# Recurrent part of a decoder: full three-pass output product, second norm and shifted term on ScalarE, channel mix added by an accumulating DMA

## The reference

```python
x = layernorm(x, ln0_w, ln0_b)
for l in range(4):
    h = layernorm(x, ln1_w[l], ln1_b[l]); hh = time_shift(h)
    xk, xv, xr = (h * t + hh * (1 - t) for t in (tmk[l], tmv[l], tmr[l]))
    k, v, sr = xk @ Wk[l].T, xv @ Wv[l].T, sigmoid(xr @ Wr[l].T)
    x = x + (sr * wkv(time_decay[l], time_first[l], k, v)) @ Wo[l].T
    h = layernorm(x, ln2_w[l], ln2_b[l]); hh = time_shift(h)
    xk, xr = (h * t + hh * (1 - t) for t in (cmk[l], cmr[l]))
    kf = square(relu(xk @ Wck[l].T))                  # 256 -> 1024
    x = x + sigmoid(xr @ Wcr[l].T) * (kf @ Wcv[l].T)  # 1024 -> 256
```

## Time and profile before

| | |
|---|---|
| runs | median 1903.39 us of 3 (1900.92 to 1904.49) |
| profiled execution | 1903.27 us, its span 1901.6 us |
| mean granted clock of PE | 0.97 of 2.4 GHz |
| busy in the span | PE 93%, PEld (weight loads) 80%, DVE 65%, ACT 44%, POOL 0% |

### The profile page before, as it was taken

How to read it: one execution, slowest core, us unless ns; L and a number is a source line. 1 busy time by engine, 2 the same in 40 slices (tenths; PEclk the granted TensorE clock), 3 DMA queues, 4 the chain that set the end, 5 groups by cost and what they waited for, 6 DMA issues and landing times.

```text
span 1901.6 us, 26356 instructions
## 1 busy us (share of the span) xinstructions
PE 1777.8 (93%) x10124; PEld 1527.4 (80%) x10124; DVE 1233.4 (65%) x1953; ACT 841.2 (44%) x1304; POOL 3.6 (0%) x26
## 2 busy tenths in 40 slices
PE   2399999999999988889799999999999999999997
PEld 1277787877787767788789899889998898998896
DVE  6889999989999943788644445445445444454445
ACT  3465676665667634344332333333333323333333
POOL 0000000000000000000000000000000000000000
PEclk9699999999999998899899999999999999999999
DMA  3000001001001002111021111011100001011001
GB/s 111 5 23 17 10 25 40 6 8 43 17 12 50 1 0 88 52 43 37 10 77 34 34 34 34 0 33 33 33 33 0 33 33 33 33 34 38 1 1 39
DMA packets 35274, 56.54 MB, mean 30 GB/s; under 512 B 3094, under 2 KB 20476, under 8 KB 34684
## 3 DMA queue, kind: packets, MB, share of 16 engines
q1 hardware_dynamic: 35196, 55.47, 9.0%
HBM read 51.79 MB, written 3.67 MB: 29 GB/s over the span
## 4 chain that ended last, share of the span: by engine, by line
PE 49%; DVE 1%; ACT 0%; issue 0%; ACTq 0%; DVEq 0%
PE fbanks L1662 16%; PE fbank L1662 16%; PE fbank L1678 16%; DVE acc L1517 0%; DVE fst L1543 0%; PE fbank L52 0%; DVE xk L1541 0%; ACT acc L1633 0%; PE fbanks L1695 0%; ACT acc L1610 0%; DVE fmv L1546 0%; DVE fyy L1557 0%; DVE frstd L1558 0%; DVE fyy L1556 0%; ACTq L1340 0%
## 5 line engine op out<-in xcount | busy, mean ns | idle before, releaser
L1493 DVE TENSOR_TENSOR hf<-sil,fbanks 128x512 f32<-128x512 f32 (+1 forms) x128 | 79.4, 620 | 332.1 <-PE fbanks L1662 273.4
L1601 ACT ACTIVATE sil<-fbanks 128x512 f32<-128x512 f32 (+1 forms) x128 | 69.6, 544 | 442.2 <-PE fbanks L1662 442.2
L1678 PE MATMUL fbank<-wl,hh 128*128 128x256 f32 x896 | 250.3, 279 | 0.0
L1678 PE MATMUL fbank<-wh,hl 128*128 128x256 f32 x896 | 250.1, 279 | 0.0
L1678 PE MATMUL fbank<-wh,hh 128*128 128x256 f32 x896 | 250.1, 279 | 0.0
L1493 DVE TENSOR_TENSOR hf<-sil,fbank 128x512 f32<-128x512 f32 (+1 forms) x128 | 79.5, 621 | 149.8 <-PE fbank L1662 142.8
L715 PE MATMUL pair<-wcv,kf 128*112 128x256 f32 x768 | 176.1, 379 | 0.0
L1678 PEld LDWEIGHTS fbank<-wl,hh 128*128 128x128 f32 x896 | 168.3, 188 | 2.2
L1678 PEld LDWEIGHTS fbank<-wh,hh 128*128 128x128 f32 x896 | 168.4, 188 | 1.8
L1678 PEld LDWEIGHTS fbank<-wh,hl 128*128 128x128 f32 x896 | 168.4, 188 | 0.0
L1500 DVE TENSOR_TENSOR hl<-hf,hh 128x512 fp32r<-128x512 f32 (+1 forms) x256 | 158.3, 618 | 0.0
(11 more groups left out here) (237 smaller groups left out, 3478.3 us busy)
## 6 DMA issues: line engine op xcount, KB each, us to landing
raw<-in_w_gate SPq DMA_DIRECT2D x16, 512.0 KB, 3.8
raw<-in_w_up SPq DMA_DIRECT2D x16, 512.0 KB, 4.7
raw<-in_w_down SPq DMA_DIRECT2D x16, 512.0 KB, 5.6
raw<-in_w_ck SPq DMA_DIRECT2D x4, 1024.0 KB, 4.8
wcv<-in_w_cv SPq DMA_DIRECT2D x4, 768.0 KB, 4.4
raw<-in_ctx_t SPq DMA_DIRECT2D x4, 750.0 KB, 6.4
ct<-in_ctx_t SPq DMA_DIRECT2D x4, 750.0 KB, 5.0
x<-in_x SPq DMA_DIRECT2D x4, 448.0 KB, 6.2
```

Source lines behind the costliest of these rows:

```text
L1493: dve.tensor_tensor(hf[i][:, 0:w], sil[i][:, 0:w], bank[2 * i + 1][:, 0:w], ALU.mult).then_inc(hf_ready, 1)
L1601: act.activation(sil[f % 2][:, 0:w], bank[2 * (f % 2)][:, 0:w], ACT.Silu).then_inc(sil_ready, 1)
L1678: ins = pe.matmul(bank[4 + 2 * (t % 2) + i // 2][:, (i % 2) * C:(i % 2 + 1) * C], a[t % 2][:, f, i * P:(i + 1) * P], m[h][:, DOWN + f * C: ...
```

## The change

- The output product takes three passes over all eight blocks, and its loop goes by pairs of blocks instead of by sequences: two of the four pairs, the first turn, two pairs. All four `hidden` groups get a high part on ACT and a low part on DVE; `w_cv` goes through the stage buffer as a whole, and half its value is what is split.
- The second norm's four scalings move from DVE to ACT (`normalise(2, ...)`, with a shift computed by DVE).
- The difference of the second mix is gone: ACT writes the previous token's term (`past`, scaled by `1 - mu`), and DVE adds the present token's in one op each (`mix2`).
- `add_channel` is gone: GpSimd issues an accumulating DMA of `cth` onto the tokens, and the semaphore `x_done` counts by 16. ACT's `gate` of the next step and DVE's statistics of the first norm wait for it.
- On ACT, DVE and PE the order changes: `wkv_numerator` moves ahead of the first mix, and the splits of the weights move to other places of a layer's first step.

Its core, in the order GpSimd, SP, DVE, ACT, PE:

```diff
+            for m in range(STEPS):
+                c = m % GROUPS
+                pool.wait_ge(cq_done, 2 * (m + 1))
+                pool.dma_start(x[:, c * G:(c + 1) * G, :], cth[:], accum_op=ALU.add).then_inc(x_done, 16)
...
                 w = io["w_" + name][l].rearrange("p b c -> p (b c)")
-                if name == "cv":
-                    w = w[:, 0:SPLIT * C]
                 sp.dma_start(stage[:, 0:w.shape[1]], w).then_inc(stage_in, 16)
...
             for s in range(-3, STEPS + 1):
                 if valid(s):
                     after(add_wkv(s))
                     stats(2, chunk(s))
-                    if s % GROUPS == 0:
-                        l = s // GROUPS
-                        low_weights(2 * l, wckl, wckh, ck_done, 4 * GROUPS * l)
+                if valid(s - 1):
+                    low_kf(s - 1, 3)
                 if valid(s + 1):
                     wkv_denominator(s + 1)
                 if valid(s):
                     rsqrt(2, s)
-                    normalise(2, xn[2], chunk(s), xn_ready[2])
+                    set_shift(2)
+                if valid(s + 1):
+                    wkv_numerator(s + 1)
                 if valid(s + 2):
-                    n = difference(1, s + 2)
-                    mix(1, s + 2, ("k", "v", "r"), ("tmk", "tmv", "tmr"), mix1_ready, n)
+                    mix1(s + 2)
                 if valid(s):
-                    n = difference(2, s)
-                    mix(2, s, ("cr",), ("cmr",), mix2_ready, n)
+                    mix2(s, 0, "cr", "cmr")
                 if valid(s - 1):
                     gate_channel(s - 1)
                 if valid(s):
-                    mix(2, s, ("ck",), ("cmk",), mix2_ready, n)
-                if valid(s + 1):
-                    wkv_numerator(s + 1)
-                if valid(s - 1):
-                    add_channel(s - 1)
+                    mix2(s, 1, "ck", "cmk")
                 if valid(s):
                     low_ck(s)
+                    if s % GROUPS == 0:
+                        l = s // GROUPS
+                        low_weights(2 * l, wckl, wckh, ck_done, 4 * GROUPS * l)
...
-                if valid(s) and s % GROUPS == 0:
-                    l = s // GROUPS
-                    low_weights(2 * l + 1, wcvl, wcvh, cv_done, 2 * GROUPS * l)
...
                 if valid(s):
                     low_kf(s, 0)
+                if valid(s):
+                    low_kf(s, 1)
+                if valid(s + 2):
+                    wkv_sums(s + 2)
+                if valid(s):
+                    if s % GROUPS == 0:
+                        l = s // GROUPS
+                        low_weights(2 * l + 1, wcvl, wcvh, cv_done, 2 * GROUPS * l)
+                    low_kf(s, 2)
...
+            def past(m, i, name, mu):
+                act.wait_ge(h_ready[2], CB * (m + 1))
+                if m:
+                    act.wait_ge(*((cr_done, m) if name == "cr" else (ck_done, 4 * m)))
+                for b in range(CB):
+                    act.activation(mixed[name][:, b], h[2][:, b, :, 0:T], ACT.Copy, scale=param(m, b, mu))\
+                        .then_inc(past_ready, 1)
...
                 act.wait_ge(square_done, 4 * m + j + 1)
-                if m and j == 0:
-
-                    act.wait_ge(cv_done, 2 * m)
-                act.activation(kfh[:, 2 * j:2 * j + 2], t[:], ACT.Copy).then_inc(kfh_ready, 1)
+                act.activation(kfh[:, 2 * j:2 * j + 2], t, ACT.Copy).then_inc(kfh_ready, 1)
...
                 if valid(s):
                     gate(s)
+                    if s % GROUPS == 0:
+                        l = s // GROUPS
+                        high_weights(2 * l + 1, wcvh, cv_done, 2 * GROUPS * l)
...
-            def channel_out(m, sequences):
...
+            def channel_out(m, pairs):
+                for p in pairs:
+                    pe.wait_ge(kfl_ready, FT // 2 * m + p + 1)
+                    for i in range(G):
+                        for f in range(2):
+                            j = 2 * p + f
+                            for n, (a, w) in enumerate(((kfh[:, j], wcvh), (kfh[:, j], wcvl), (kfl[p][:, f], wcvh))):
+                                ins = pe.matmul(pair[3][0:T, i // 2, (i % 2) * C:(i % 2 + 1) * C],
+                                                a[:, i * T:(i + 1) * T], w[:, j * C:(j + 1) * C],
+                                                start=j == n == i % 2 == 0,
+                                                stop=j == FT - 1 and n == 2 and i % 2 == 1)
...
                     pe.wait_ge(wlo_ready, 2 * (m // GROUPS) + 2)
-                    pe.wait_ge(w_in["cv"], 16 * (m // GROUPS + 1))
                     pe.wait_ge(cth_ready, m + 1)
-                    channel_out(m, (0, 1, 2))
+                    channel_out(m, (0, 1))
...
-                    channel_out(m, (3,))
+                    channel_out(m, (2, 3))
```

More of the change, by code:

```diff
@@ L103, in rwkv_phase @@
         wckh, wckl = sb("wckh", [P, CB * F], F32R), sb("wckl", [P, CB * F], F32R)
-        wcvh, wcvl = sb("wcvh", [P, SPLIT * C], F32R), sb("wcvl", [P, SPLIT * C], F32R)
-        wcv = sb("wcv", [P, (F // P - SPLIT) * C])
+        wcvh, wcvl = sb("wcvh", [P, FT * C], F32R), sb("wcvl", [P, FT * C], F32R)
         prm = sb("prm", [P, L, CB, NPRM])
@@ L137, in rwkv_phase @@
         bb = sb("bb", [P, CB, G, T1])
[L138 to L140 removed]
+        ckh = sb("ckh", [P, CB, G * T], F32R)
+        with nc.sbuf_tensor("mix_ck", [P, CB, G, T], FP32) as t:
+            mixed["ck"] = t
+        ckl = sb("ckl", [P, CB, G * T], F32R)
+        with nc.sbuf_tensor("kf", [P, FT, G * T], FP32) as t:
+            kf = [t[:, 2 * j:2 * j + 2] for j in range(FT // 2)]
+        t = sb("kfl", [P, FT, G * T], F32R)
+        kfl = [t[:, 2 * j:2 * j + 2] for j in range(FT // 2)]
+        kfh = sb("kfh", [P, FT, G * T], F32R)
         cth = sb("cth", [T, G, C])
@@ L407, in low_weights @@
                     dve.wait_ge(used, count)
-                dve.tensor_tensor(tile[:], stage[:, 0:tile.shape[1]], high[:], ALU.subtract).then_inc(wlo_ready, 1)
+                dve.scalar_tensor_tensor(tile[:], stage[:, 0:tile.shape[1]], 0.5 if n % 2 else 1.0, high[:], ALU.mult,
+                                         ALU.subtract).then_inc(wlo_ready, 1)
             def gate_channel(m):
@@ L621, in _ @@
                 if valid(s):
+                    past(s, 1, "ck", "pmk")
+                    if s % GROUPS == 0:
+                        l = s // GROUPS
+                        high_weights(2 * l, wckh, ck_done, 4 * GROUPS * l)
                     high_ck(s)
@@ L699, in hidden @@
                 ins.then_inc(ck_done, 1)
-            def channel_out(m, sequences):
-                for i in sequences:
-                    n = 0
-                    for j in range(F // P):
-                        if i == 0 and j % 2 == 0 and j < SPLIT:
-                            pe.wait_ge(kfl_ready, SPLIT // 2 * m + j // 2 + 1)
-                        elif i == 0 and j % 2 == 0:
-                            pe.wait_ge(square_done, 4 * m + j // 2 + 1)
-                        if j < SPLIT:
-                            parts = [(a[:, j], w[:, j * C:(j + 1) * C]) for a, w in ((kfh, wcvh), (kfh, wcvl), (kfl, wcvh))]
-                        else:
-                            parts = [(kf[j // 2][:, j % 2], wcv[:, (j - SPLIT) * C:(j - SPLIT + 1) * C])]
-                        for a, w in parts:
-                            ins = pe.matmul(pair[3][0:T, i // 2, (i % 2) * C:(i % 2 + 1) * C], a[:, i * T:(i + 1) * T],
-                                            w, start=n == 0, stop=j == F // P - 1)
-                            n += 1
-                    if i % 2:
-                        ins.then_inc(cv_done, 1)
+            def channel_out(m, pairs):
[9 more added lines that the diff above has]
+                                                stop=j == FT - 1 and n == 2 and i % 2 == 1)
+                        if i % 2 and p == FT // 2 - 1:
+                            ins.then_inc(cv_done, 1)
             for s in range(-3, STEPS + 1):
```

154 lines of the change are left out of this document (69 added, 85 removed).

## The result

The changed kernel takes 1936.05 us (median of 4 runs, 1933.73 to 1936.81), the kernel before 1903.94 in the same comparison; the ratio is 1.0169, 95% interval 1.0151 to 1.0186. The profiled execution took 1933.73 us with a span of 1931.6, 30.0 more than the span before.

The account below looks back on a forecast made before the run. PE (TensorE) alone was taken to set the 40.52 us recurrent step. From 1903.27 us, nine ordinary steps -4.2, four layer starts +36 and ends -0.7 gave 1934 us, own range 1918 to 1948 (1911 to 1968 with part of the rivals).

Parts of the forecast that it names:

- The turn comes late: First turn, ordinary step: PE waits 1.4 us for ScalarE's `xn`, so the step takes 40.05 instead of 40.52 us.
- the product's saving: Output product on PE: 1.85 us less work per step, of which an ordinary step keeps only 0.47.
- The second turn holds by 0.2: Second turn: second norm's `xn` ready at H + 26.8, PE there at H + 27.0, so moving that norm costs nothing.
- The DMA is hidden: Accumulating DMA of `cth`: taken as 6.2 us, hidden up to 7.7 us in ordinary steps.
- The layer starts: Weight splits at a layer's first step, four times: the main cost, +9.0 us per layer, +36 in four.
- H': H is the first matmul of a step's hidden product; H' is the next step's, put at H + 40.05.
- the load: The 1 MB `wcv` load at a layer start: 4.8 us, landing at H' + 3.9, ScalarE waiting for it at `wcvh`.
- the half product: Half of the output product, 5.7 us; after PE's wait at a layer start its slower records add 2.4.
- PE's wait for `wcvl`: Output product at a layer start: PE wants `wcvl` at H' + 13.3, ready at H' + 21.9, a stall of 8.6 us.
- Ordinary steps: Nine recurrent steps without a layer start: 0.47 us less each, -4.2 in all.
- the fill: First steps of the recurrent part: PE waits for VectorE anyway, so the change there is 0.
- the ends: Fill 0, last three steps -1.9 us each, +5 at the very end waiting for the DMA: together -0.7.

Follow-up runs that it names:

- experiment 7: Changed kernel with only the order within a step altered on ScalarE and VectorE, shortening the chains to both turns; weight splits stay: 1914.73 us.
- experiment 5: Changed kernel with each accumulating DMA followed by a plain one of the same size into unused memory: 1970.58 us.
- experiment 6: Changed kernel with `xn` of the first norm made ahead of the two `eu` operations on ScalarE, nothing else moved: 1943.03 us.
- experiment 4: Changed kernel without the accumulating DMA; VectorE adds the channel mix's result to the tokens again: 1928.32 us.
- experiment 1: Changed kernel with the low split of the `wcv` weights (`wcvl`) on VectorE moved ahead of the first hidden group's low part: 1923.05 us.
- experiment 2: Changed kernel with an own stage buffer for the `wcv` weights, loaded early; order on every engine stays: 1924.36 us.
- experiment 3: Changed kernel with the own `wcv` stage buffer and `wcvl` ahead of the first hidden group's low part: 1909.58 us.
- experiment 10: Changed kernel with experiments 1, 2, 7 and 8 together, and the last of sixteen accumulating DMAs replaced by two VectorE adds: 1872.45 us, ratio 0.9832.
- experiment 11: On top of experiment 10, the `wcv` low split made by GpSimd in two operations instead of by VectorE: 1894.15 us.
- experiment 8: On top of experiment 3, ScalarE makes the `wcv` high split (`wcvh`) right behind `ckh` instead of behind the gate: 1907.97 us.

## Why the prediction was right, and where it was not

The mechanism was right in its parts, and the time, 1934 against 1936.05, closer than its terms were.

*The turn comes late.* Forecast: a wait of 1.4, a step of 40.05. Measured 1.3 and 40.05. That the product's saving is real is shown by experiment 7, that ScalarE's chain eats it by 5 and 6.

*The second turn holds by 0.2.* `xn` of the second norm ends at 397.93 in the ordinary step that begins at 380.96, PE takes it at 397.98: 0.05 is left over, and in experiment 6 PE waits there.

*The DMA is hidden.* Taken as 6.2 us, it lands after 5.2; in ordinary steps no one waits for it, and experiment 4 changes no step. The fit in the Trainium skill (DMA: Bandwidth & Descriptors, Anatomy of one DMA) gave an estimate of 3.1; the accumulating DMA of this case disagrees (5.2), while the plain copy of the same bytes in experiment 5 took 3.6.

*The layer starts.* `wcvl` was ready 22.0 us behind H' (281.08 to 303.12), forecast 21.9; the load was late by 2.4, forecast 2.5; the half product took 2.2 more on average, forecast 2.4. The step's two ends:

```profile
281.08 0.76 PE L701 MATMUL pair<-ckh,wckh 128*128 128x448 f32 x2
...
331.02 0.76 PE L701 MATMUL pair<-ckh,wckh 128*128 128x448 f32 x2
```

PE's wait for `wcvl` was 7.5 and not 8.6, mostly because PE came later than forecast: the hidden product ahead took 0.9 longer, since the stuck ScalarE emptied its banks late, which the forecast did not have. The one makes up for the other, and from H to H the four steps take 49.3, 49.9, 48.7 and 49.5, forecast 49.5. The term was still too large, +36 for +32.8: I compared with an ordinary step of before, but the kernel before has its own layer starts, 41.4 from H to H in three of the four layers (41.53 from `wo` to `wo`, in the row shown above), which I had not read. Experiments 1 to 3 show that order and load are the cause, and that neither is enough alone; both together take 25.4 of the 32.8 away.

*Ordinary steps, fill and tail.* From H to H, nine ordinary steps gave 4.6 (forecast 4.2). Forecast for the fill 0, for the ends -0.7. The changed kernel comes 2.2 earlier to its first H, unforeseen; the last three steps and the end together gave -0.6, with the DMA at 5.8 (experiment 4) for the 5 that I had set.

*What was not in the sum.* The 4.5 us behind the recurrent part, at a lower granted clock in code that is the same. Their cause stays open. The length of PE's pause ahead of the attention part does not decide it: in experiments 10 and 11 the pause is 6.8 us in both, and the first 55.5 us behind it have clocks of 0.85 and 0.78; in experiment 5 it is 17.7, the longest, and yet what comes behind the recurrent part takes 1157.0 us as in the kernel before (1157.1; the changed kernel 1161.7). Around the start of the experts the clock is 0.66 to 0.69 in all changed kernels but that one, which has the 0.75 of before. Windows of the kernel before, the changed one and experiment 5, from 166.5 to 222 us behind the start of the attention part:

```profile
910.97:966.47 55.50, 45.27 (x257) 41.42 (x256) 31.26 (x55) 20.99 (x34) 0.10 (x1) 0.75 0.23 74
936.41:991.91 55.50, 45.47 (x238) 41.62 (x237) 29.75 (x53) 19.25 (x30) 0.10 (x1) 0.66 0.23 74
978.80:1034.30 55.50, 45.37 (x257) 41.53 (x257) 31.25 (x54) 21.11 (x34) 0.10 (x1) 0.75 0.23 74
```

So the stretch can be as fast in a changed kernel too, and executions of the kernel before differ by as much (1900.94 to 1907.64 in the twelve beside experiments 1 to 4). The hit within 2 us is therefore in part luck: a layer term that was 3 too large, and 2.2 of the fill, against 4.5 that no term held.

## What to carry to other kernels

When a change makes one engine's work shorter, look for the chain on another engine that ends at the same place, and ask for its slack in us; here 1.85 us on TensorE became 0.47, until the chains were reordered, and then 2.06. A larger preparation step that runs once per layer has to be placed as carefully as the loop: what it waits for (one stage buffer for two loads), what it is queued behind, and whether its engine is full in that very stretch. And subtract what the same place already costs before.

## What the runs showed of the hardware that I had not expected

Whether PE's clock falls after a short wait is not the same each time, even for the same wait at the same place. After waits of 4.5 and 7.5 us the step's clock was below 1.00 in every layer (experiment 1, the changed kernel). Of the four waits of 3.0 in experiment 3 three were followed by a step at 0.96 and one by a step at 1.00; of the four of 2.6 in experiment 8 it was two and two.

VectorE operations with two inputs in SBUF stood still beside GpSimd (experiment 11), but only some: the one at 272.04, across the end of the one GpSimd operation and the start of the next, ran in 1.09. The Trainium skill (SBUF — State Buffer, SBUF: two separate sides) states that such an operation and one of GpSimd that reads SBUF exclude each other, and that the one that starts first holds the port to its end; the second pair agrees, 273.24 + 5.34 ends 0.95 us, about the operation's own time, behind 272.88 + 4.75. The first does not quite: 267.48 + 4.53 ends 0.8 us ahead of the recorded end of the GpSimd operation that started before it, 266.13 + 6.67.
